# A graph layer with a gated update and a small expert layer: the weights' own product moved to the program's start, one gate's product moved at the first node tiles, and a new order for the last tile

## The chip, the cores and the metric

One Trainium2 chip, one of its cores. The metric is the time of one execution in microseconds (us); lower is better.

## What is computed

x has 10000 rows of 512; there are 2500 edges with 128 attributes each, sorted by destination. The reference, cut to what matters:

```python
hn = _layernorm(x)
m = relu(concatenate([hn[src], edge_attr], axis=1) @ W1.T + b1) @ W2.T + b2
agg = segment_sum(m, dst, num_segments=10000)
gi = agg @ W_ih.T + b_ih
gh = hn @ W_hh.T + b_hh
r = sigmoid(i_r + h_r); z = sigmoid(i_z + h_z); n = tanh(i_n + r * h_n)
h_new = (1.0 - z) * n + z * hn
x = x + hn + batchnorm(h_new)
h2 = _layernorm(x)
x = x + top2_of_8_experts(h2) + 0.5 * shared_expert(h2)
```

## The kernel before, in words

Every product keeps float32 accuracy with three matmuls: each operand is split into a high part (ScalarE, ACT, copies it to the fast format) and a low part (VectorE, DVE, subtracts), and TensorE (PE) multiplies high by high, high by low and low by high. One matmul of PE has 512 columns; a product over 512 inputs is 12 matmuls.

**Edges.** The 2560 padded edges are 20 tiles of 128, in 5 groups g of 4 tiles j. Per group: GpSimd (POOL) gathers the source rows (`gather_source`, L703), DVE takes their statistics (`stats`), POOL and ACT normalise them (`front`, `normalise`), PE turns them (`transposes`, L1271), ACT and DVE split them (`transposed_hi`, `transposed_lo`), PE makes the first layer (`layer1`, L1283, 60 matmuls per group), DVE adds b1 (`messages`), and PE sums edges of one destination with a 0/1 matrix (`sums`, L1334). W2 and W_ih are not applied one after the other: `fused_weights` (L1303) multiplies W2 by W_ih once, 3 thirds q of 4 tiles i by 12 matmuls, and b2 by W_ih, 3 times 12 matmuls. `product(g, j)` (L1352) multiplies the sums by the result and DVE adds what earlier tiles left (`take_gates`, L1031). `find` and `find_before` (L1035, L1039) search all destinations for each edge's own, `last_places` turns that into addresses. `keep_running` (L1371) issues turns of the identity, whose result nobody reads.

**Nodes.** 79 tiles t of 128 rows, a pipeline of periods (`periods`, L479): in period p, PE makes gates r, n and z of tile t, the expert layers of tiles t-1 (`f1`, 296 columns, 12 matmuls) and t-2 (7 matmuls of 512 columns). A chain runs from the z gate over DVE (five steps and the statistics, L1670 to L1680), POOL and ACT to the turn of tile t's rows by PE in the next period.

**What sets the order.** Each engine has its own instruction list, written out by hand, and runs it in order; semaphores (`wait_ge`) tie them. SP's list of DMA issues (L611 to L627) sets the order of the loads, POOL's list that of the gathers.

## Time and profile before

| | |
|---|---|
| three runs | 1315.44, 1317.50, 1317.52 us (median 1317.5) |
| profiled execution | 1315.33 us, its span 1313.5 us |
| PE busy | 1280.1 us (97%), 6360 matmuls |
| DVE, POOL, ACT busy | 997.5, 819.8, 732.8 us (76, 62, 56%) |
| mean DMA rate | 137 GB/s |

The busy time of PE is the time in which a matmul was under way; 97% leaves some 33 us of the span in which none was. In the page's 40 slices PE shows 6 tenths in the first, 5 in the last, and 8 or 9 in the others.

### The profile page before, as it was taken

What the parts mean: (1) busy time and instruction counts of PE and PEld (TensorE: products, weight loads), DVE (VectorE), ACT (ScalarE), POOL (GpSimd) and SP (SyncE); (2) the same over time, 40 slices, a digit from 0 to 9 for tenths busy, and PEclk for the clock granted to TensorE, in tenths of its full rate; (3) what the DMA queues carried; (4) which work ended last, traced back from release to release, by engine and by line L of the source; (5) the groups of instructions that cost most, each with busy time, mean ns of one, the idle gap of its engine ahead of it and who ended that gap; (6) DMA issues with size and microseconds to landing.
All of it is one profiled execution on the core that took longest, in us unless ns stands there. A gap on an engine that the chain in (4) does not pass through costs nothing. (4 is left out here: it accounts for less than half of the span.)

```text
span 1313.5 us, 22819 instructions
## 1 busy us (share of the span) xinstructions
PE 1280.1 (97%) x6360; PEld 1082.6 (82%) x6360; DVE 997.5 (76%) x2190; ACT 732.8 (56%) x1721; POOL 819.8 (62%) x1119
## 2 busy tenths in 40 slices
PE   6999999999899999999999999999999999999995
PEld 5788888888688888888888888888888888888884
DVE  6887666659687777778778778777777777877874
ACT  4420223124576666666666666666666666666652
POOL 4201152213787777777777777777778777777761
PEclk9999999999899999999999999999999999999998
DMA  8213554277434334334344343333333333433320
GB/s 328 59 33 113 177 211 172 112 276 241 144 122 132 132 126 134 123 128 136 120 131 133 122 138 123 129 135 126 132 125 128 136 120 130 134 121 136 126 97 33
DMA packets 62960, 179.58 MB, mean 137 GB/s; under 512 B 9360, under 2 KB 10000, under 8 KB 62800
## 3 DMA queue, kind: packets, MB, share of 16 engines
q1 hardware_dynamic: 46912, 99.20, 21.9%
q0 software_dynamic: 16016, 79.97, 18.0%
q8 instruction: 17, 0.28, 0.1%
q14 instruction: 15, 0.12, 0.0%
HBM read 141.86 MB, written 37.29 MB: 136 GB/s over the span
## 5 line engine op out<-in xcount | busy, mean ns | idle before, releaser
L1737 PE MATMUL bank<-whh_hi,x_hi 128*128 128x512 f32 x948 | 376.3, 397 | 0.4 <-DVE g_out L1029 0.4
L1737 PE MATMUL bank<-whh_hi,x_lo 128*128 128x512 f32 x948 | 369.9, 390 | 0.0
L1737 PE MATMUL bank<-whh_lo,x_hi 128*128 128x512 f32 x948 | 369.5, 390 | 0.0
L1737 PEld LDWEIGHTS bank<-whh_hi,x_lo 128*128 128x128 f32 x948 | 177.9, 188 | 37.9
L1737 PEld LDWEIGHTS bank<-whh_hi,x_hi 128*128 128x128 f32 x948 | 178.2, 188 | 35.8 <-issue 0.8
L1737 PEld LDWEIGHTS bank<-whh_lo,x_hi 128*128 128x128 f32 x948 | 178.3, 188 | 34.4
L1535 POOL TENSOR_TENSOR h_n<-h,n_gate 128x512 f32<-128x512 f32 x78 | 100.9, 1294 | 65.5 <-ACT n_gate L1586 65.5
L1467 POOL TENSOR_TENSOR rstd<-var_eps,minus_half 128x1 f32<-128x1 f32 x158 | 89.9, 569 | 66.9 <-DVE var_eps L499 66.9
L1634 DVE TENSOR_TENSOR h_lo<-bank,h_hi 128x512 fp32r<-128x512 f32 x79 | 54.6, 692 | 80.8 <-ACT h_hi L1577 80.8
L1452 POOL DMA_INDIRECT gates<-gates_in,slot_at x78 | 84.2, 1079 | 45.8 <-issue 45.8
L1529 POOL TENSOR_TENSOR n_pre<-r_hn,gates 128x512 f32<-128x512 f32 x78 | 100.5, 1288 | 13.2 <-POOL r_hn L1525 13.2
L1777 PE MATMUL bank<-f_hi,h_hi 128*128 128x296 f32 x316 | 102.1, 323 | 2.3 <-DVE h_lo L1634 2.3
L541 POOL TENSOR_TENSOR x_lo<-x_lo_raw,x_hi 128x512 fp32r<-128x512 f32 x77 | 100.7, 1308 | 2.9 <-ACT x_hi L535 0.4
L1517 POOL TENSOR_TENSOR x_h_b<-x_h,bn_shift 128x512 f32<-128x512 f32 x78 | 101.1, 1296 | 0.0
L1525 POOL TENSOR_TENSOR r_hn<-r_gate,hn 128x512 f32<-128x512 f32 x78 | 99.7, 1279 | 1.8 <-DVE hn L1610 1.3
L1777 PE MATMUL bank<-f_lo,h_hi 128*128 128x296 f32 x316 | 95.4, 302 | 0.0
...
L1777 PE MATMUL bank<-f_hi,h_lo 128*128 128x296 f32 x316 | 95.3, 301 | 0.0
L1366 PE MATMUL bank<-wih_hi,a_hi 128*128 128x512 f32 x240 | 93.9, 391 | 0.0
L1366 PE MATMUL bank<-wih_lo,a_hi 128*128 128x512 f32 x240 | 93.4, 389 | 0.0
L1366 PE MATMUL bank<-wih_hi,a_lo 128*128 128x512 f32 x240 | 93.4, 389 | 0.0
L1577 ACT ACTIVATE h_hi<-bank 128x512 fp32r<-128x512 f32 x79 | 47.4, 600 | 75.6 <-PE bank L546 75.5
...
## 6 DMA issues: line engine op xcount, KB each, us to landing
...
```

What stands on the lines that cost most here:

```text
L541: eng.tensor_tensor(x_lo[:, s, :], x_raw[:, s, :], x_hi[:, s, :].bitcast(F32), ALU.subtract)\
L1366: last = pe.matmul(to[0:R, :], a[:, k, j * R:(j + 1) * R], w[:, k, q * D:(q + 1) * D], start=n == 0, stop=n == 3 * DK - 1)
L1452: pool.indirect_dma_start(out=gates[:, s, :], out_offset=None, in_=gates_in, in_offset=bass.IndirectOffsetOnAxis(ap=slot_at[:, s:s + 1], a ...
L1467: pool.tensor_tensor(rstd[which][:, of:of + 1], var_eps[which][:, :], minus_half[0:R, 0:1], ALU.pow)\
L1517: pool.tensor_tensor(x_h_b[:, s, :], x_h[:, s, :], bn_shift[:, :], ALU.add).then_inc(x_h_b_done, 1)
L1525: pool.tensor_tensor(r_hn[:, :], r_gate[:, :], hn[:, s, :], ALU.mult).then_inc(r_hn_done, 1)
L1529: pool.tensor_tensor(n_pre[:, :], r_hn[:, :], gates[:, s, 2 * D:G3], ALU.add).then_inc(n_pre_done, 1)
L1535: pool.tensor_tensor(h_n[:, :], h[:, s, :], n_gate[:, s, :], ALU.subtract).then_inc(h_n_done, 1)
L1577: act.activation(h2_hi[:, :], b_th2[:, 0:DK * R], ACT.Copy).then_inc(h2_hi_done, 1)
L1634: dve.tensor_tensor(h2_lo[:, :], b_th2[:, 0:DK * R], h2_hi[:, :].bitcast(F32), ALU.subtract)\
L1737: last = pe.matmul(to[0:R, :], a[:, s, k * R:(k + 1) * R], w[:, k, q * D:(q + 1) * D], start=n == 0, stop=n == 3 * DK - 1)
L1777: last = pe.matmul(b_f1[0:R, 0:F1], a[:, k * R:(k + 1) * R], w[:, k, 0:F1], start=n == 0, stop=n == 3 * DK - 1)
```

## The change

Line numbers of the change are its own. It has three parts.

**Start.** PE's list begins with 12 turns of the identity and the product of the weights (its first third in quarters over k, each as its loads come), and the first edge rows are gathered, normalised and turned beside it; `fused_weights` is gone from its place behind `layer1(1)`. W2 and the first third of W_ih come in four quarters of 256 KB each, as SP's first loads; W1 comes last. POOL makes the identity first and gathers after the quarters have landed. PSUM banks are dealt out anew. ACT's and DVE's lists follow: the searches stand between other work, two of them ahead of the first rows' low parts. The waits on PE's list are new too.

**Third node tile.** Its 12 matmuls of gate r stand behind tile 1's gate z, ahead of the turning of tile 0's new rows, and no longer behind tile 0's first expert layer.

**Last tile.** DVE, not POOL, makes its r*hn and the sum before tanh; ACT makes its tanh ahead of two older steps; `best_two` and the choice of experts of tile 77 stand behind the last tile's chain, and the y of tile 76 one period later; PE turns the identity 25, 10 and 6 times between; the last 7 matmuls become 14 of 256 columns in two banks, and y is added and stored in halves.

DVE's list at the start, as it now stands:

```python
    for k in range(DK):
        quarters_lo(k)
    ...
    third_lo(1)
    for of in HALVES:
        stats(0, of)
    third_lo(2)
    fused_lo(0)
    dve.wait_ge(dst_in, 16)
    ...
    dve.wait_ge(all_dst_in, 16)
    ...
    dve.tensor_copy(all_dst[:, 0:E], all_dst_i[:, :]).then_inc(all_dst_done, 1)
    ...
    find(0)
    find(1)
    for j in range(SUP):
        transposed_lo(0, j)
    w1_lo_of(0, slice(0, 3))
    fused_lo(1)
    w1_lo_of(1, slice(3, K1))
    attributes_lo(0)
    stats(1)
    compare(0)
    fused_lo(2)
    messages(0, 0)
    ...
    find_before(0)
    messages(0, 1)
    messages_lo(0, 0)
    find_before(1)
    find_before(2)
    messages(0, 2)
    messages_lo(0, 1)
    messages(0, 3)
    messages_lo(0, 2)
    messages_lo(0, 3)
    attributes_lo(1)
    for j in range(SUP):
        transposed_lo(1, j)
    count(0)
    sums_lo(0)
    compare(1)
    messages(1, 0)
    find(2)
    messages(1, 1)
    messages_lo(1, 0)
    ...
```

ACT's list at the start up to the second group's messages, as it now stands:

```python
    for k in range(DK):
        act.wait_ge(fused_in[k], 32)
        hi_of(w2_hi[:, k, :], w2_raw[:, k, :]).then_inc(w_hi_done, 1)
        hi_of(wih_hi[:, k, 0:D], wih_raw[:, k, 0:D]).then_inc(wih_hi_done, 1)
    third_hi(1)
    act.wait_ge(b_in, 32)
    hi_of(b2_hi[:, :, :], b2_col[:, :].unsqueeze(2).broadcast_to((P, DK, P))).then_inc(w_hi_done, 1)
    third_hi(2)
    for of in HALVES:
        normalise(0, of)
    v_of(0)
    fused_hi(0)
    for n, at in enumerate((slice(0, 3), slice(3, K1))):
        act.wait_ge(w1_in[n], 16)
        hi_of(w1_hi[:, at, :], w1_raw[:, at, :]).then_inc(w_hi_done, 1)
    attributes_hi(0)
    for j in range(SUP - 1):
        transposed_hi(0, j)
    v_of(1)
    transposed_hi(0, SUP - 1)
    fused_hi(1)
    v_of(2)
    normalise(1)
    fused_hi(2)
    for j in range(SUP):
        messages_hi(0, j)
    attributes_hi(1)
    for j in range(SUP):
        transposed_hi(1, j)
    for f in range(DK):
        sums_hi(0, f)
    ...
```

The rest, cut to its core:

```diff
def bank_of_rows(g, j):
-        return bank[2 + (j if g < 2 else j % 2)]
+        return bank[((0, 1, 2, 0), (4, 5, 2, 3))[g][j] if g < 2 else 2 + j % 2]
+
+    def bank_of_units(g, j):
+        return bank[j % 2 + (6 if g == 0 else 0)]
...
@@ -609,22 +618,22 @@
     sp.dma_start(src_i[:, :], src).then_inc(src_in, 16)
+    for k in range(DK):
+        sp.dma_start(w2_raw[:, k, :], w2v[:, k, :]).then_inc(fused_in[k], 16)
+        sp.dma_start(wih_raw[:, k, 0:D], wihv[:, k, 0:D]).then_inc(fused_in[k], 16)
+    sp.dma_start(wih_raw[:, :, D:2 * D], wihv[:, :, D:2 * D]).then_inc(third_in[0], 16)
+    sp.dma_start(b2_col[:, :], b2).then_inc(b_in, 16)
+    sp.dma_start(b1_row[:, :], bcast(b1)).then_inc(b_in, 16)
+    sp.dma_start(wih_raw[:, :, 2 * D:G3], wihv[:, :, 2 * D:G3]).then_inc(third_in[1], 16)
+    sp.wait_ge(xs_in[SUP - 1], 16)
+    sp.dma_start(dst_i[:, :], dst).then_inc(dst_in, 16)
+    sp.dma_start(all_dst_i[:, :], dst_back.broadcast_to((R, E))).then_inc(all_dst_in, 16)
     sp.dma_start(w1_raw[:, 0:3, :], w1v[:, 0:3, :]).then_inc(w1_in[0], 16)
     sp.dma_start(m_raw[:, K1 - 1, :], attr_t[:, 0:SW]).then_inc(attr_in, 16)
     sp.dma_start(w1_raw[:, 3:K1, :], w1v[:, 3:K1, :]).then_inc(w1_in[1], 16)
-    sp.wait_ge(xs_in[SUP - 1], 16)
-    sp.dma_start(b1_row[:, :], bcast(b1)).then_inc(b1_in, 16)
-    sp.dma_start(dst_i[:, :], dst).then_inc(dst_in, 16)
-    sp.dma_start(w2_raw[:, :, :], w2v).then_inc(w2_in, 16)
     sp.dma_start(row_i[:, :], dst_rows[0:1, :].broadcast_to((R, SW))).then_inc(row_in, 16)
-    sp.dma_start(b2_col[:, :], b2).then_inc(b2_in, 16)
-    for k in range(2):
-        sp.dma_start(wih_raw[:, k, :], wihv[:, k, :]).then_inc(wih_in[k], 16)
     sp.dma_start(ig_bias[:, :], bcast(b_ih)).then_inc(bias_in, 16)
     sp.dma_start(ig_bhh[:, :], bcast(b_hh[0:2 * D])).then_inc(bias_in, 16)
-    for k in range(2, DK):
-        sp.dma_start(wih_raw[:, k, :], wihv[:, k, :]).then_inc(wih_in[k], 16)
-    sp.dma_start(all_dst_i[:, :], dst_back.broadcast_to((R, E))).then_inc(all_dst_in, 16)
...
-    pool.wait_ge(src_in, 16)
-    for j in range(SUP):
-        gather_source(0, j)
...
+    pool.wait_ge(src_in, 16)
+    pool.wait_ge(fused_in[DK - 1], 32)
+    for j in range(SUP):
+        gather_source(0, j)
...
+        if g == 0:
+            pe.wait_ge(fused_lo_done, DK)
+            if j == SUP - 1:
+                pe.wait_ge(t_lo, 1)
+        elif g == 1:
+            pe.wait_ge(fused_lo_done, 2 * DK if j < 2 else 3 * DK)
+        else:
...
+            if j < 2 and g == 0:
+                pe.wait_ge(fused_lo_done, 2 * DK)
+            elif j < 2:
+                pe.wait_ge(a_lo_done, DK * (g - 1) + j + 1)
+    def first_third():
+        for k in range(DK):
+            for n, (a, w) in enumerate(((w2_hi, wih_hi), (w2_hi, wih_lo), (w2_lo, wih_hi))):
+                if n == 0:
+                    pe.wait_ge(w_hi_done, k + 1)
+                    pe.wait_ge(wih_hi_done, k + 1)
+                if n == 1:
+                    pe.wait_ge(w_lo_done, k + 1)
+                    pe.wait_ge(wih_lo_done, k + 1)
+                for i in range(DK):
+                    last = pe.matmul(bank_of_fused(0, i)[:, :], a[:, k, i * P:(i + 1) * P], w[:, k, 0:D],
+                                     start=k == 0 and n == 0, stop=k == DK - 1 and n == 2)
+                    if k == DK - 1 and n == 2:
+                        last.then_inc(fused_prod, 1)
+    def third(q, tiles=range(DK)):
+        for i in tiles:
+            if i == 0:
+                pe.wait_ge(wih_lo_done, DK + q)
+            if q == 1 and i == DK - 1:
+                pe.wait_ge(fused_hi_done, 1)
+            if q == 2 and i == 0:
+                pe.wait_ge(t_lo, SUP)
+            if q == 2 and i == 2:
+                pe.wait_ge(fused_hi_done, 2 * DK + 3)
...
+    def bias_times_wih(q):
+        pe.wait_ge(w_lo_done, DK + 1)
+        if q > 0:
+            pe.wait_ge(wih_lo_done, DK + q)
+        if q == 1:
+            pe.wait_ge(fused_lo_done, DK)
+        if q == 2:
+            pe.wait_ge(t_lo, SUP - 1)
...
+        if g == 0:
+            pe.wait_ge(fused_lo_done, 3 * DK)
...
-    keep_running(14)
+    keep_running(12)
+    first_third()
+    bias_times_wih(0)
+    third(1)
+    for j in range(SUP - 1):
+        transposes(0, j)
+    bias_times_wih(1)
+    transposes(0, SUP - 1)
+    bias_times_wih(2)
+    third(2)
+    layer1(0)
     for j in range(SUP):
-        transposes(0, j)
-    keep_running(8)
-    layer1(0)
-    for j in range(2):
         transposes(1, j)
     sums(0)
-    for j in range(2, SUP):
-        transposes(1, j)
     layer1(1)
-    fused_weights()
     for j in range(SUP):
         product(0, j)
...
-    store(NT - 1, (NT - 1) % 2)
+    for n in range(2):
+        sp.wait_ge(y_done, NT + n)
+        sp.dma_start(out_tiles[:, NT - 1:NT, HALF[n]].rearrange("p o d -> p (o d)"),
+                     y[:, (NT - 1) % 2, HALF[n]]).then_inc(y_stored[(NT - 1) % 2], 16)
...
+    def last_new_gate(dve, p):
+        t, s = p.t, p.slot(1)
+        dve.wait_ge(r_done, t + 2)
+        dve.wait_ge(hn_done, t + 2)
+        dve.wait_ge(n_pre_done, t + 1)
+        dve.tensor_tensor(r_hn[:, :], r_gate[:, :], hn[:, s, :], ALU.mult).then_inc(r_hn_done, 1)
+        dve.wait_ge(n_done, t + 1)
+        dve.wait_ge(gates_loaded[s], 16 * (p.turn(1) + 1))
+        dve.wait_ge(r_hn_done, t + 2)
+        dve.tensor_tensor(n_pre[:, :], r_hn[:, :], gates[:, s, 2 * D:G3], ALU.add).then_inc(n_pre_done, 1)
...
+        if p.last(-1):
+            s = p.slot(-3)
+            dve.wait_ge(f2_prod, t - 2)
+            dve.wait_ge(y_stored[s], 16 * p.turn(-3))
+            dve.tensor_tensor(y[:, s, :], b_f2[0:R, :], x1[:, p.slot4(-3), :], ALU.add).then_inc(y_done, 1)
...
+        if p.last(0):
+            best_two(dve, p)
...
+            if p.last(1):
+                last_new_gate(dve, p)
+        if p.has(-2) and not p.last(0):
+            if p.last(-2):
+                for n, product in enumerate((b_f2, b_n)):
+                    dve.wait_ge(f2_prod, t - 1 + n)
+                    dve.tensor_tensor(y[:, s, HALF[n]], product[0:R, HALF[0]], x1[:, p.slot4(-2), HALF[n]],
+                                      ALU.add).then_inc(y_done, 1)
...
+    def second_layer(to, n, of):
+        for k in range(KF - 1):
+            for a, w in ((hid_hi, f2_hi), (hid_hi, f2_lo), (hid_lo, f2_hi)):
+                pe.matmul(to[0:R, 0:n], a[:, k * R:(k + 1) * R], w[:, k, of],
+                          start=k == 0 and a is hid_hi and w is f2_hi, stop=False)
+        last = pe.matmul(to[0:R, 0:n], hid_hi[:, (KF - 1) * R:KF * R], f2_hi[:, KF - 1, of],
+                         start=False, stop=True)
+        last.then_inc(f2_prod, 1)
+    def reset_gate(pe, p, k):
+        t, s = p.t + k, p.slot(k)
+        pe.wait_ge(x_lo_done, t + 1)
+        wait_from(pe, r_pre_done, t - 1)
+        gate(s, b_r[s], 0).then_inc(r_prod, 1)
+
     def body(p):
         t = p.t
         if p.has(0):
             s = p.slot(0)
-            pe.wait_ge(x_lo_done, t + 1)
-            wait_from(pe, r_pre_done, t - 1)
-            gate(s, b_r[s], 0).then_inc(r_prod, 1)
+            if not p.first(-2):
+                reset_gate(pe, p, 0)
             wait_from(pe, hn_done, t)
             gate(s, b_n, 2).then_inc(n_prod, 1)
         if p.has(0):
             if p.first(-1):
                 gate(p.slot(0), z_bank(p), 1).then_inc(z_prod, 1)
+
+                reset_gate(pe, p, 1)
...
+        if p.last(-1):
+            keep_running(10)
...
+            if p.last(-2):
+                second_layer(b_f2, D // 2, HALF[0])
+                second_layer(b_n, D // 2, HALF[1])
+            else:
+                second_layer(b_f2, D, slice(0, D))
+        if p.last(0):
+            pe.wait_ge(hn_done, NT)
+            pe.wait_ge(h_new_done, NT)
+            keep_running(8)
+            pe.wait_ge(x1_done, NT)
+            keep_running(6)
+            pe.wait_ge(var_done[2], NT)
+            keep_running(11)
+        if p.last(-1):
+            keep_running(6)
```

PE's list at the program's start. Before (ident is the identity, xs the gathered rows, w and m the first layer's operands):

```order
L1374 MATMUL bank<-ident 128x128 x14
L1279 MATMUL bank<-ident,xs 128x128 x16
L1374 MATMUL bank<-ident 128x128 x8
L1298 MATMUL bank<-w_hi,m_hi 128x512
L1298 MATMUL bank<-w_lo,m_hi 128x512
```

Now (wih and w are W_ih and W2):

```order
L1425 MATMUL bank<-ident 128x128 x12
L1344 MATMUL bank<-wih_hi,w_hi 128x512 x4
L1344 MATMUL bank<-wih_lo,w_hi 128x512 x4
L1344 MATMUL bank<-wih_hi,w_lo 128x512 x4
L1344 MATMUL bank<-wih_hi,w_hi 128x512 x4
```

The first layer and the turning of rows gave their place to 48 matmuls on weights alone, in four quarters of three such groups.

DVE's list around the first rows' low parts (m_lo). Before:

```order
L937 TENSOR_TENSOR w_lo<-w_lo_raw,w_hi 128x1024
L937 TENSOR_TENSOR m_lo<-m_lo_raw,m_hi 128x512
L962 TENSOR_TENSOR m_lo<-bank,m_hi 128x4x128 x4
L937 TENSOR_TENSOR w_lo<-w_lo_raw,w_hi 128x2048
L1116 CAST dst_f<-dst_i 128x20
L1117 CAST gval<-dst_i 128x8x2
L988 TENSOR_TENSOR msg_lo_raw<-bank,b_row 128x512
```

Now (wih_lo<-bank is the low part of the weights' product, found a search's result):

```order
L954 TENSOR_TENSOR wih_lo<-wih_lo_raw,wih_hi 128x4x512
L1024 TENSOR_TENSOR wih_lo<-bank,wih_hi 128x512 x4
L1143 CAST dst_f<-dst_i 128x20
L1144 CAST gval<-dst_i 128x8x2
L1148 CAST all_dst<-all_dst_i 128x2560
L1149 COPY all_dst<-dst_f 128x20
L1060 MAX_INDEX found<-dst_f,all_dst 128x8 x2
L986 TENSOR_TENSOR m_lo<-bank,m_hi 128x4x128 x4
L954 TENSOR_TENSOR w_lo<-w_lo_raw,w_hi 128x1536
```

The destinations' cast over 2560 columns and two searches stand ahead of the first m_lo now; the messages are far behind.

PE's list at its end, from the last whole period's second layer. Before:

```order
L1787 MATMUL bank<-f_hi,hid_lo 128x512
L1789 MATMUL bank<-f_hi,hid_hi 128x512
L546 MATMUL bank<-ident,h_169 128x128 x4
L546 MATMUL bank<-ident,hid 128x128 x3
L1777 MATMUL bank<-f_hi,h_hi 128x296
L1777 MATMUL bank<-f_lo,h_hi 128x296
```

Now (b_n takes the turns of the identity):

```order
L1857 MATMUL bank<-f_hi,hid_lo 128x512
L1859 MATMUL bank<-f_hi,hid_hi 128x512
L1852 MATMUL bank<-ident 128x128 x25
L552 MATMUL bank<-ident,h_169 128x128 x4
L1852 MATMUL bank<-ident 128x128 x10
L552 MATMUL bank<-ident,hid 128x128 x3
L1907 MATMUL bank<-f_hi,h_hi 128x296
L1907 MATMUL bank<-f_lo,h_hi 128x296
```

Twenty-five turns of the identity stand where the list had none, and ten more stand between the last tile's turn and that of hid.

## Rows read from the trace of the kernel before

**Rows 1.** Waits of PE over the whole span: total us, times, longest
```profile
PE bank L546 <- ACT h L1568: 10.3, 3, 5.5
PE bank L1374 <- POOL minus_half L746: 9.3, 1, 9.3
PE bank L1346 <- DVE msg_lo L993: 1.3, 1, 1.3
```

**Rows 2.** Windows: length, busy us (x) of PE, PEld, DVE, ACT, POOL, clock, DMA, GB/s
```profile
0.00:17.60 17.60, 6.93 (x38) 6.06 (x39) 7.80 (x19) 8.70 (x11) 10.96 (x27) 1.00 0.71 244
34.20:322.00 287.80, 287.60 (x1356) 240.97 (x1356) 205.78 (x317) 74.00 (x128) 57.53 (x65) 1.00 0.43 151
338.80:348.90 10.10, 4.22 (x17) 3.84 (x17) 5.04 (x10) 5.25 (x12) 7.30 (x9) 0.66 0.37 130
348.90:1289.30 940.40, 940.05 (x4775) 798.79 (x4774) 742.31 (x1776) 622.12 (x1528) 725.65 (x993) 1.00 0.38 126
1289.30:1302.50 13.20, 6.89 (x27) 5.85 (x26) 7.13 (x20) 2.82 (x11) 1.01 (x3) 0.74 0.05 20
```

**Rows 3.** Timeline of the first weight load, one window's rate, a DMA issue to landing
```profile
1.18 0.42 SPq L612 DMA_DIRECT2D w_lo_raw<-in_w1t  x1
...
5.78 1.48 ACT L809 ACTIVATE w_hi<-w_lo_raw 128x1536 fp32r<-128x1536 f32 x1 [3.76 <-DMA w_lo_raw<-in_w1t]
...
6.00:8.00 2.00, 0.00 (x0) 0.00 (x0) 0.71 (x1) 1.39 (x2) 1.58 (x3) 1.00 1.06 421
...
all_dst_i<-in_dst_back SPq DMA_DIRECT2D x1, 1280.0 KB, 18.9
```

**Rows 4.** Timeline of PE at the start: start us, us, instruction [idle before]
```profile
9.26 3.25 PE L1374 MATMUL bank<-ident 128*128 128x128 f32 x14 [9.26 <-POOL minus_half L746]
...
30.88 0.39 PE L1298 MATMUL bank<-w_lo,m_hi 128*128 128x512 f32 x1
31.11 0.39 PE L1298 MATMUL bank<-w_hi,m_lo 128*128 128x512 f32 x1
```

**Rows 5.** Timeline of DVE: rows' low parts, the destinations' cast and one search
```profile
16.79 2.48 DVE L962 TENSOR_TENSOR m_lo<-bank,m_hi 128x512 fp32r<-128x512 f32 x4 [2.30 <-ACT m_hi L825]
...
71.33 1.49 DVE L1164 CAST all_dst<-all_dst_i 128x2560 f32<-128x2560 int32 x1
...
73.13 2.82 DVE L1036 FIND_INDEX8 found<-dst_f,all_dst 128x8 uint32<-128x2560 f32 x1
```

**Rows 6.** Timeline of PE, POOL and DVE at the first node tiles
```profile
338.45 1.29 POOL L541 TENSOR_TENSOR x_lo<-x_lo_raw,x_hi 128x512 fp32r<-128x512 f32 x1
...
343.19 1.11 PE L546 MATMUL bank<-ident,h 128*128 128x128 f32 x4 [4.37 <-ACT h L1568]
...
347.18 1.29 POOL L1535 TENSOR_TENSOR h_n<-h,n_gate 128x512 f32<-128x512 f32 x1 [0.74 <-ACT n_gate L1586]
...
350.23 0.68 DVE L1670 TENSOR_TENSOR bank<-bank,h_n 128x512 f32<-128x512 f32 x1
```

**Rows 7.** Timeline of PE, ACT and DVE over the last tiles
```profile
1285.91 0.38 PE L1777 MATMUL bank<-f_hi,h_hi 128*128 128x296 f32 x1
...
1294.94 1.12 PE L546 MATMUL bank<-ident,h 128*128 128x128 f32 x4 [5.53 <-ACT h L1568]
...
1297.47 0.61 PE L1777 MATMUL bank<-f_hi,h_hi 128*128 128x296 f32 x1 [0.77 <-DVE h_lo L1634]
...
1286.58 0.62 ACT L1586 ACTIVATE n_gate<-n_pre 128x512 f32<-128x512 f32 x1
...
1287.83 0.47 DVE L1653 TENSOR_TENSOR bank<-bank,f_bias 128x296 f32<-128x296 f32 x1 [0.68 <-PE bank L1777]
...
1288.95 0.68 DVE L1670 TENSOR_TENSOR bank<-bank,h_n 128x512 f32<-128x512 f32 x1
...
1300.84 0.47 DVE L1653 TENSOR_TENSOR bank<-bank,f_bias 128x296 f32<-128x296 f32 x1 [3.09 <-PE bank L1777]
...
1307.77 0.69 DVE L1725 TENSOR_TENSOR y<-bank,x 128x512 f32<-128x512 f32 x1 [2.00 <-PE bank L1789]
```

318 lines of the change are left out of this document (147 added, 171 removed).

## The prediction

> **What bounds the kernel now.** I read the waits of TensorE (PE) first, then busy time by stretch, then timelines of the three places that the change touches. From 34.2 to 322 us PE had 287.6 of 287.8 us busy, and from 348.9 to 1289.3 us 940.05 of 940.4 [rows 2]: there the time is PE's own work, which the change keeps. What it can give back are the places where PE has nothing to do. There are three [rows 1, 2]: the start (idle to 9.26 us, then dummy turns and short waits), the first node tiles (338.8 to 348.9 us: 4.2 of 10.1 us busy, mean clock 0.66), and the last tile (from 1289.3 us: 6.9 of 13.2 busy, clock 0.74). The sum is made against the profiled execution, 1315.33 us; 0.2%, about what a measurement of this kernel can tell from no change, is 2.6 us.
>
> **The start, before.** The first first-layer matmul starts at 17.6 us. Ahead of it PE did one useful thing, 16 turns of 128 columns. Fourteen dummies took 3.25 us, 0.23 each [rows 4]; the second of the two levels, 2.4 GHz against 1.2, is twice as fast, so the 16 are worth about 1.6 us. Lost: 17.6 - 1.6 = 16.0 us. A later wait for msg_lo, between the rows' turning and the sums, adds 1.3 [rows 1].
>
> **The start, after.** PE's real work begins once a quarter of W2 and of W_ih is there and split. The first load of before, 768 KB, was issued at 1.18 us and its reader began at 5.78; the rate was then 421 GB/s [rows 3]. A quarter pair is 512 KB in two issues, 256 KB less: 0.6 us earlier, 5.1 us. ACT then makes two high parts of 512 columns at 0.6 each (n_gate, the same shape, took 0.62 [rows 7]): PE starts at 6.3 us. The further pairs come every 512 KB / 421 GB/s = 1.25 us, ACT needs 1.2 for one, DVE as much (four m_lo of 512 columns took 2.48, 0.62 each [rows 5]), PE 12 x 0.227 = 2.7 us (matmuls of 512 columns start 0.23 apart [rows 4]): PE is the slowest, so after its first quarter it should not wait. PE started at 9.26 on the lower level before; now the dummies start at about 2 us, since POOL makes the identity before the gathers. After the pause at 343 us the lower level lasted until the next stretch, some 6 us [rows 2, 6]; so I take it until 8 us: half of 8 - 6.3, 0.9 us, is lost. Lost at the start: 7.2 us in place of 16.0, a gain of 8.8.
>
> Eight loads now stand where one stood. The Trainium skill ("DMA: Bandwidth & Descriptors", section "Anatomy of one DMA — SWDGE (gpsimd) path") gives each DMA about 2.0 us fixed plus its bytes at 436 GB/s. The trace speaks against paying the fixed part one after the other: three loads of 1.5 MB issued within 1.4 us kept 421 GB/s between 6 and 8 us [rows 3]. By that page's figures, paid serially, the fourth pair would land at about 22 us; the same mechanism, priced from rows, is rival B.
>
> **New waits of the start.** PE has 48 + 12 + 48 matmuls (24.5 us) ahead of its first row turns: it comes to them at 6.3 + 0.9 + 24.5 = 31.7 us. Gathers, statistics and normalisation of the first rows were done before 17.6 us; starting 6 us later, they end by about 24, hidden. The gathers' DMAs pass behind 2 MB of quarters and beside 2 MB of thirds: at 421 GB/s all of it is in by about 17 us. SP waits for the last gather, then issues the destinations' table (1280 KB, 3.1 us at that rate), in by about 22; W1 follows by 27 and is needed from 37. DVE has about 27 us of work and waits until the product's first low parts are made (after ACT's copies, which stand behind the rows' normalisation); then the cast, 1.5, and two searches, 2.8 each [rows 5], to 34.3, then the rows' low parts, 0.6 each: the third at 36.2. PE has made three tiles' turns, b2's second product (2.7) and the fourth tile's turn by 35.9 and waits for that third part with b2's third product: 0.3 to 0.9, I take 0.5. The sums of the first group wait for the last message's low part as before, with 16 turns ahead of them and not 8: 0.8 in place of the 1.3. The next first layer follows the sums at once; its bank waits for DVE's a_lo, behind four m_lo, a count and the attributes, whose load can only be issued when the first layer is done: 0.4. No wait in the products: DVE's rest there (12 double additions, 4 searches, 4 m_lo, `last_places`) is some 32 us beside 33 us of PE, and four banks let PE lead by 10 us. Start in all: 8.8 + 1.3 - 1.7 = **8.4 us**. Bounds: 10 with no new wait and the quarters 0.6 sooner; 4 with the quarters 3 us later and double waits.
>
> **The third node tile.** PE waited 4.37 us for tile 0's new rows, until 343.19. The third tile's x_lo ends at 339.74 [rows 6], so its 12 matmuls (2.7 us) fit in from 339.8 to 342.6. What they free behind the first expert layer is PE's time, though, and the next bound is the chain: POOL's h_n of tile 1 starts at 347.18 for 1.29 us, whatever PE does, and DVE's step on it, at 350.23 before, can start at 348.5 [rows 6]. PE then waits for tile 1's chain twice. So of 2.7 us and of what the higher clock gives (the first expert layer at half the time), 350.23 - 348.5 = **1.7 us** comes through. Bounds: -0.5, if the clock falls in the new pauses, and 2.7.
>
> **The last tile.** DVE needs 0.7 for each of the two steps that POOL took 1.29 for (h_n shows POOL's rate [rows 6]); it can begin when ACT has r. Two such steps are 1.2 us shorter, and ACT's tanh, at 1286.58 before, can be at 1285.1, behind h_hi; but DVE's z_pre slips behind y and h_lo (0.7 each, three in a row from 1285.0), so the sigmoid on it ends at about 1287.7 and the chain starts at 1287.75 in place of 1288.95 [rows 7]: 1.2. PE's turn of the new rows comes at 1293.7, not 1294.94. From there to the first expert matmul were 2.53 us, at the lower clock (four turns 1.12); kept awake by dummies, with DVE's hid of tile 77 now ahead of h_lo, about 2.35: 1296.05 in place of 1297.47. Twelve matmuls and the hand-over to DVE took 3.37 us at the lower clock and 1.92 in the period before [rows 7]: DVE's bias starts at 1297.97 in place of 1300.84, 2.87 us sooner. From there to y the work is the same. Halving the 7 matmuls changes no columns; the last addition has 256 columns, about half of 0.69 [rows 7], so 0.3 less, and the last store half the bytes, 0.1: **3.3 us**. The dummies cost nothing while they fit into the pauses: 25 x 0.1 us between 1289.7 and 1293.7, 10 behind the turn beside 1.9 us of ACT and DVE; at 0.23 each the ten would delay the product by 0.3 to 0.8. Bounds: 0.5 and 4.5.
>
> **Sum.** 8.4 + 1.7 + 3.3 = 13.4: 1315.33 - 13.4 = 1301.9 us for an execution like the profiled one. The median of the runs lies 2.2 above it, two of three at 1317.5; between the two I put the new median at 1302.5.
>
> **Rivals.**
> - A, dummies that do not keep the clock. They fill about half of the pause, and nothing in the trace shows dummies holding it; before, the turns at 1294.94, after 5.5 us of nothing, were slow (1.12 for four) [rows 7]. If it falls, the product is at half speed as before and ten cold dummies stand ahead of it: the last tile gives 1.2 - 0.5 + 0.4 = 1.1: 1304.7. The Trainium skill ("TensorE: Matmul & The Clock Gate", section "What's actually happening") says that the gate follows how busy PE has been lately, which would favour the dummies.
> - B, quarters paid one after another, each pair 5.1 - 1.2 = 3.9 us: the fourth lands at 16.8 us, PE ends the first third at 20.7 in place of 18.1, and the second third, 4.6 us for its load and 4.4 for its parts, keeps PE waiting for 2.4 more: 5 us, 1307.5. Against it stands the rate [rows 3].
> - C, slower: the table of destinations lands late. DVE's list holds the cast ahead of everything that PE needs from the rows. The place is the third part for which b2's third product waits. From about 27 us on, each us of delay is one of the whole. Before, this load took 18.9 us to land, with some 6 MB queued ahead [rows 3]; issued at 18 it would be in at 37, which costs 10: 1312.5. Past 43 us the change is slower than before, at 45 it gives 1320. Against it: 17 us is when the queue ahead is empty.
> - D, more than forecast: no new wait, quarters early, whole r product saved: 10 + 2.7 + 4.5 = 17.2, 1298.7.
>
> **Chances.** Forecast with its bounds 0.72, A 0.10, B 0.05, C 0.08 (0.04 of it slower than before), D 0.05. Faster by over 0.2%: 0.93; within 0.2%: 0.03; slower: 0.04. The range reaches from just under D past B, to a table that lands 7 us late (C): 1298 to 1309.5.
>
> **What would show it.** Right: PE's first product matmul at 6 to 7 us and no idle over 1 us in it; L1374's wait of 9.3 us gone, waits of under 1 us for m_lo, msg_lo and a_lo; no r product behind the first expert layer, h_n of tile 1 followed by DVE at once, and PE waits of 1 to 2 us in the third tile; clock 1.00 from the last turn to the end. Wrong: a wait of PE for m_lo over 2 us (C), the second quarter's matmuls waiting for ACT (B), clock 0.5 in the last expert layer (A), or PE's stretch of products no longer full.

## The result, and the profile after

| | kernel before | changed kernel |
|---|---|---|
| median of runs | 1317.16 us (5 runs, 1315.44 to 1317.52) | 1305.45 us (5 runs, 1303.76 to 1308.08) |
| ratio after / before | | 0.9916, 95% interval 0.9898 to 0.9933 |
| profiled execution, and its span | 1315.33, 1313.5 us | 1303.76, 1301.9 us |

The change is 11.7 us faster by the medians and 11.6 by the profiled executions, where 15.0 (from the three runs' median of 1317.5 to 1302.5) and 13.4 were forecast. The new runs lie 4.3 us apart, and the profiled one is the fastest of them.

Waits of TensorE (PE) in the changed kernel (us in total, times, longest), which answer to [rows 1]:

```profile
PE bank L552 <- ACT h L1648: 2.1, 3, 1.4
PE bank L1344 <- ACT wih_hi L820: 2.1, 1, 2.1
PE bank L1907 <- DVE h_lo L1733: 2.0, 2, 1.5
PE bank L1844 <- DVE x L1774: 1.6, 1, 1.6
PE bank L552 <- POOL hid L1569: 1.5, 2, 1.2
PE bank L1378 <- DVE m_lo L986: 0.6, 1, 0.6
PE bank L1306 <- DVE m_lo L986: 0.3, 1, 0.3
```

The wait of 10.3 us for h is 2.1, the one of 9.3 us for the identity has gone, and two small waits for m_lo are new. The windows of the changed kernel (length, PE busy, clock, DMA share, GB/s) answer to [rows 2]:

```profile
0.00:17.60 17.60, 13.98 (x53) 1.00 0.90 307
34.00:60.00 26.00, 25.09 (x114) 1.00 0.15 43
330.00:350.00 20.00, 14.68 (x72) 1.00 0.33 109
1280.00:1297.00 17.00, 12.83 (x90) 1.00 0.09 36
```

The clock column tells nothing of the time before the first rise; from there it holds 1.00 to the last product, through the places where it was 0.66 and 0.74 [rows 2]. The timeline of PE (start, us, instruction, idle before it) shows the start; its first rows answer to [rows 4]:

```profile
1.54 2.82 PE L1425 MATMUL bank<-ident 128*128 128x128 f32 x12 [1.54 <-POOL minus_half L752]
6.45 2.04 PE L1344 MATMUL bank<-wih_hi,w_hi 128*128 128x512 f32 x4 [2.09 <-ACT wih_hi L820]
8.29 1.91 PE L1344 MATMUL bank<-wih_lo,w_hi 128*128 128x512 f32 x4
10.00 1.18 PE L1344 MATMUL bank<-wih_hi,w_lo 128*128 128x512 f32 x4
...
37.39 0.63 PE L1306 MATMUL bank<-ident,xs 128*128 128x128 f32 x4 [0.34 <-DVE m_lo L986]
38.59 0.47 PE L1378 MATMUL bank<-wih_hi,b_hi 128*128 128x512 f32 x1 [0.57 <-DVE m_lo L986]
```

The eight first products take 1.84 and 1.71 us per four, as on the lower level; from 10.0 on four start within 1.0, then 0.91. From the node stage and the tail, rows that answer to [rows 6, 7], first DVE's (VectorE's) steps on the first tiles and on tile 77 in the kernel before, then the changed kernel's:

```profile
327.98 0.75 DVE L1610 SCALAR_TENSOR_TENSOR hn<-bank,rstd,hn_bias 128x512 f32<-128x512 f32 x1 [0.48 <-PE bank L1737]
...
337.17 0.70 DVE L1670 TENSOR_TENSOR bank<-bank,h_n 128x512 f32<-128x512 f32 x1
...
1276.74 0.68 DVE L1670 TENSOR_TENSOR bank<-bank,h_n 128x512 f32<-128x512 f32 x1
```
```profile
321.16 0.75 DVE L1685 SCALAR_TENSOR_TENSOR hn<-bank,rstd,hn_bias 128x512 f32<-128x512 f32 x1 [1.16 <-PE bank L1844]
...
329.82 0.70 DVE L1766 TENSOR_TENSOR bank<-bank,h_n 128x512 f32<-128x512 f32 x1
...
341.25 0.70 DVE L1766 TENSOR_TENSOR bank<-bank,h_n 128x512 f32<-128x512 f32 x1
...
1267.78 0.68 DVE L1766 TENSOR_TENSOR bank<-bank,h_n 128x512 f32<-128x512 f32 x1
...
1285.00 0.65 PE L552 MATMUL bank<-ident,h 128*128 128x128 f32 x4 [0.33 <-ACT h L1648]
1285.49 1.25 PE L1852 MATMUL bank<-ident 128*128 128x128 f32 x10
1287.05 0.52 PE L552 MATMUL bank<-ident,hid 128*128 128x128 f32 x3 [0.31 <-POOL hid L1569]
...
1289.24 0.47 DVE L1710 TENSOR_TENSOR bank<-bank,f_bias 128x296 f32<-128x296 f32 x1 [0.68 <-PE bank L1907]
...
1294.23 0.39 PE L1857 MATMUL bank<-f_hi,hid_hi 128*128 128x256 f32 x1 [1.04 <-DVE hid_lo L1752]
```

Where the 11.6 us came from, by the same instructions in both profiles: the node stage's first step on DVE (line 1685) starts at 321.16 instead of 327.98, so the start gave 6.8. DVE's step on tile 0's h_n is at 329.82 instead of 337.17, 7.35 sooner. That further 0.5 is no part of the change at the third tile: DVE waited 1.72 us for the gates of its first tile to land, and 2.49 before. The step on tile 1's h_n, 350.23 [rows 6], is at 341.25, 8.98 sooner: the third tile gave 1.6. Tile 77's step is 8.96 sooner, so the tiles between gave nothing. The last bias addition went from 1300.84 [rows 7] to 1289.24, 11.6 sooner: the last tile gave 2.6, and nothing behind it gave anything.

### The profile page after: what moved, and what is told of

Same layout as the page of the kernel before. It is cut to its first block and busy times, and to the rows that moved or that the text cites. A ratio compares the mean times of both kernels' runs of the same rounds, so it can differ in the third digit from the quotient of the medians.

```text
span 1301.9 us, 22928 instructions
## 1 busy us (share of the span) xinstructions
PE 1281.2 (98%) x6398; PEld 1083.2 (83%) x6398; DVE 997.7 (77%) x2198; ACT 734.0 (56%) x1726; POOL 816.4 (63%) x1117
## 5 line engine op out<-in xcount | busy, mean ns | idle before, releaser
L1844 PEld LDWEIGHTS bank<-whh_lo,x_hi 128*128 128x128 f32 x948 | 178.3, 188 | 34.3
L1575 POOL TENSOR_TENSOR x_h_b<-x_h,bn_shift 128x512 f32<-128x512 f32 x78 | 101.2, 1297 | 0.0
## 6 DMA issues: line engine op xcount, KB each, us to landing
whh_lo_raw<-in_whh_t SPq DMA_DIRECT2D x4, 768.0 KB, 10.3
```

The costliest lines, as they stand in the source:

```text
L1575: pool.tensor_tensor(x_h_b[:, s, :], x_h[:, s, :], bn_shift[:, :], ALU.add).then_inc(x_h_b_done, 1)
L1844: last = pe.matmul(to[0:R, :], a[:, s, k * R:(k + 1) * R], w[:, k, q * D:(q + 1) * D], start=n == 0, stop=n == 3 * DK - 1)
```

## The experiments

Medians of 4 to 6 runs of each, beside runs of before on the same chip (three groups of four; the kernel before had 1317.15, 1316.59 and 1316.64 in them):

| run | median (lowest to highest) | ratio to before, 95% | clock down near 40 us / in the third tile's stretch, in its profile |
|---|---|---|---|
| e1 start undone | 1311.66 (1310.59 to 1313.20) | 0.9958 (0.9945 to 0.9972) | no / yes |
| e2 tail undone | 1308.46 (1306.65 to 1310.02) | 0.9932 (0.9919 to 0.9946) | yes / yes |
| e3 third r back | 1307.13 (1305.34 to 1308.76) | 0.9923 (0.9910 to 0.9937) | yes / yes |
| e4 transposes in the middle | 1306.53 (1304.94 to 1308.56) | 0.9920 (0.9906 to 0.9933) | yes / no |
| e5 changed kernel again | 1305.98 (1304.83 to 1307.41) | 0.9920 (0.9907 to 0.9932) | no / no |
| e6 searches behind | 1305.05 (1302.86 to 1306.16) | 0.9906 (0.9892 to 0.9921) | no / yes |
| e7 e4 and e6 together | 1302.89 (1301.56 to 1305.34) | 0.9899 (0.9884 to 0.9915) | no / no |
| e8 no transposes in the tail | 1307.82 (1306.05 to 1310.66) | 0.9932 (0.9920 to 0.9945) | yes / yes |
| e9 e7 and more at the start | 1302.51 (1301.19 to 1304.87) | 0.9895 (0.9877 to 0.9912) | no / no |
| e10 whole loads | 1307.57 (1307.22 to 1309.42) | 0.9935 (0.9921 to 0.9949) | no / no |
| e11 third's low part later | 1309.31 (1308.21 to 1310.51) | 0.9947 (0.9933 to 0.9960) | yes / yes |
| e12 last layer whole | 1304.66 (1304.33 to 1308.27) | 0.9914 (0.9898 to 0.9930) | yes / no |

The medians alone do not tell two of these versions apart when they are less than about 2 us apart: the interval of each ratio is 1.6 to 2.3 us to either side, and e1 to e4, e5 to e8 and e9 to e12 ran on three different chips. The profiles can say more, since the same stretch can be measured in each of them. The columns, in us: DVE's first step of the node stage (when it starts), from there to its step on tile 0's h_n, from tile 0's to tile 1's, from tile 1's to tile 77's, and from tile 77's to PE's first product of the last layer.

| profile | start | to tile 0 | third tile | tiles 1 to 77 | last tile |
|---|---|---|---|---|---|
| before | 327.98 | 9.19 | 13.06 | 926.5 | 29.09 |
| changed kernel | 321.16 | 8.66 | 11.43 | 926.5 | 26.45 |
| e1 | 328.10 | 9.31 | 12.54 | 927.7 | 26.04 |
| e2 | 323.27 | 9.01 | 12.64 | 926.5 | 29.07 |
| e3 | 323.58 | 8.47 | 13.10 | 927.7 | 26.41 |
| e4 | 323.55 | 9.45 | 11.46 | 927.7 | 26.41 |
| e5 | 321.63 | 9.26 | 11.45 | 927.7 | 26.45 |
| e6 | 320.29 | 9.76 | 12.51 | 927.7 | 26.41 |
| e7 | 318.31 | 9.09 | 11.47 | 927.7 | 26.42 |
| e8 | 323.46 | 8.62 | 12.64 | 927.7 | 28.75 |
| e9 | 318.50 | 8.98 | 11.44 | 927.7 | 26.42 |
| e10 | 324.51 | 9.13 | 11.44 | 926.5 | 26.41 |
| e11 | 325.36 | 8.21 | 12.17 | 926.5 | 26.41 |
| e12 | 322.82 | 9.10 | 11.45 | 927.7 | 26.42 |

The fifth column is a surprise: the 76 tiles in which PE is always busy take 926.5 us in five profiles and 927.7 in nine, at a clock of 1.00 in both, and the changed kernel has been seen with either. No experiment touched that, and its cause is open.

**e1: the start of before, with the other two parts.** The file before, with the node stage of after and its two helpers (`HALF`, `last`).

> The kernel before with the new third node tile and the new last tile, and with its own start. The two profiles give the three parts of the gain as 6.8 us (start), 2.15 us (third node tile) and 2.6 us (last tile). Theory 1, the parts stand by themselves: 4.7 us below the kernel before, about 1312.4 us, and the turn of the second tile's h at about 354 us instead of 356.2. Theory 2, the part of the start is worth the 8.4 us of the prediction and the other two are smaller than the profiles say (3.2 us together): about 1314 us. Theory 3, the later parts only pay with the new start, because the clock falls somewhere else: above 1315 us.

It ran in 1311.66 us: the other two parts are worth 5.5 us beside their own runs of before, the start 5.7 to 6.2 (to 1305.98 and 1305.45). The median is nearest to theory 1 (1312.4), so the two parts stand without the start. Its sign did not come, though: the turn of the second tile's h is at 355.96 and not at 354. In this profile the clock fell in the third tile's stretch, and that part gave 0.5 (12.54 against 13.06) and not 1.6. What the medians miss of the forecast lies mostly in the start: its 8.4 are some 6.

**e2: the old tail.**
```diff
         def last(self, k):
-            return isinstance(self.i, int) and self.t + k == NT - 1
+            return False
```
and the store of before.

> The changed kernel with the old order of the last tiles: no early choice on ScalarE, the last new gate's products on GpSimd, no transposes to keep TensorE running, the last layer and the store in one piece. Theory 1, the last tile is worth the 2.6 us that the profiles show: 1308.0 us. Theory 2, it is worth the predicted 3.3 us: 1308.8 us. Theory 3, most of it was the clock, which falls in the old tail's pause of 5.5 us and not in the new one: then the granted clock here drops before the last turns, and the last expert matmul starts 1.4 us or more after the last turn instead of the 1.2 to 2.3 us of a full clock with its dummies.

1308.46 us, 2.5 above e5 by the medians and 1.6 by the ratios, which leaves theories 1 and 2 open. The profile decides for theory 1: its last tile takes 29.07 us, as before (29.09), against 26.45. The clock also did what theory 3 says, with PE's wait of 5.53 us for h back and the four turns at 1.11:

```profile
1289.62 1.11 PE L552 MATMUL bank<-ident,h 128*128 128x128 f32 x4 [5.53 <-ACT h L1645]
```

**e3: the third tile's r at its old place.**
```diff
-                    if not p.first(-2):
-                        reset_gate(pe, p, 0)
+                    reset_gate(pe, p, 0)
...
-                        reset_gate(pe, p, 1)
```

> The changed kernel with the r product of the third node tile back behind the first tile's expert layer. Theory 1, the worth of moving it is the 2.15 us that the profiles show (predicted 1.7 us): 1307.6 us, and TensorE waits some 4 us for the first h. Theory 2, the chain of the second tile bounded the stretch in any case: within 0.5 us of the changed kernel, 1305.5 us. The clock should fall again in the longer pause, in nearly every run, which would make the runs of this kernel agree more closely than the changed kernel's five, which lie 4.3 us apart.

1307.13 us: 1.2 above e5 and 1.7 above the changed kernel's first median, 0.4 and 0.9 by the ratios. That decides between the theories as little as the intervals do. The profile does: with r at its old place, DVE's steps on tile 0's and tile 1's h_n are 13.10 us apart, as before (13.06), against 11.43 with r moved.

```profile
332.05 0.70 DVE L1766 TENSOR_TENSOR bank<-bank,h_n 128x512 f32<-128x512 f32 x1
...
345.15 0.68 DVE L1766 TENSOR_TENSOR bank<-bank,h_n 128x512 f32<-128x512 f32 x1
```

So the move is worth 1.6 to 1.7 us where the clock holds, and both theories were off. Where it falls in spite of the move (e1, e2, e6, e8, e11), the distance is 12.17 to 12.64, and the move is worth 0.4 to 0.9. PE waits 3.66 us for the first h, the window from 330 to 350 us has a clock of 0.83, and the second wait has shrunk to 0.25. The runs do not agree more closely (3.4 us apart), so the spread is not made there alone. The profile shows another place, which e2's and e4's show too: near 40 us, behind a wait for m_lo.

**e4: transposes in the middle.**
```diff
+            def fill_pause(n):
+                for _ in range(n):
+                    pe.transpose(b_thid[:, 0:P], ident[:, :], ident[:, :])
...
+                if p.first(-1):
+                    fill_pause(13)
...
+                        if p.first(-2):
+                            fill_pause(14)
                         wait_from(pe, x1_done, t)
                         gate(p.slot(0), b_z, 1, 0, 2)
+                        if p.first(-2):
+                            fill_pause(13)
```

> The changed kernel with 13, 14 and 13 transposes of the identity in three of the four pauses that TensorE still has in the third node tile's stretch (1.5, 1.6 and 1.4 us long), into the bank of the hidden units, which is free there. The changed kernel's five runs lie between 1303.8 and 1308.1 us, with mean granted clocks from 0.999 to 0.995. Theory 1, the slower ones are those in which the clock fell in these pauses: all runs here at 1303.5 to 1304.5 us. Theory 2, it falls at the start or in the tail: the same spread as before, median about 1305.4 us. Theory 3, the transposes delay the products behind them: all runs up by 0.3 to 1 us.

Theory 1 is refuted as the whole cause: the clock held in the middle, and the time did not move (0.9920, as e5). The profiled run, 1308.06 us, was over 4 slower than the changed kernel's, with no pause of PE left in the middle but 1.14 and 0.47 us. It had lost 2.4 us at the start, 0.8 until tile 0's step and 1.1 in tiles 1 to 77; the third tile took 11.46, so the transposes cost nothing there. The start's part shows in the windows of PE from 34 to 60 us, of e4 and, below it, of e3:

```profile
34.00:60.00 26.00, 23.75 (x99) 0.93 0.15 43
```
```profile
34.00:60.00 26.00, 23.74 (x99) 0.93 0.15 44
38.34 0.63 PE L1306 MATMUL bank<-ident,xs 128*128 128x128 f32 x4 [1.70 <-DVE m_lo L986]
```

0.07 of 26 us is 1.8 us, beside the 25.09 us busy at clock 1.00 in the changed kernel's profile.

**e5: the changed kernel once more.**

> The changed kernel itself, for its runs beside the others of this group on one chip. Its first five runs lay between 1303.8 and 1308.1 us. The three profiles of its variants show two places where a run can lose: TensorE's wait for the first m_lo (0.34 us in the changed kernel's profile, 1.22, 1.70 and 1.69 us in those of the variants) with a fall of the clock near 41 us behind it in those three and not in the changed kernel's own, and a fall near 342 us. Theory: the middle run has one of the two, so a median of 1305 to 1307 us again, a lowest near 1303.8, and where this profile has a wait of over 1 us for m_lo it also has the fall.

As expected in the median; its profile had the wait of over 1 us (1.17) without the fall. So the two are not one thing. Ordered by that first wait for m_lo: 0.34 and 1.17 us (the changed kernel, e5) without a fall, 1.22, 1.69, 1.70, 1.96 and 2.24 us (e2, e4, e3, e8, e12) with one.

The two profiles of this one kernel are 2.3 us apart: 0.5 at the start, 0.6 until tile 0's step and 1.1 in tiles 1 to 77, none of it a fall of the clock. The rows of tiles 1 and 77 in e5:

```profile
342.34 0.70 DVE L1766 TENSOR_TENSOR bank<-bank,h_n 128x512 f32<-128x512 f32 x1
...
1270.00 0.68 DVE L1766 TENSOR_TENSOR bank<-bank,h_n 128x512 f32<-128x512 f32 x1
```

Why m_lo is late is in DVE's timeline of e5 (and, with the same order, in all of them): from 27.10 us on it never waits until the searches are done.

```profile
27.10 2.48 DVE L1024 TENSOR_TENSOR wih_lo<-bank,wih_hi 128x512 fp32r<-128x512 f32 x4 [3.39 <-ACT wih_hi L862]
...
31.65 2.82 DVE L1060 FIND_INDEX8 found<-dst_f,all_dst 128x8 uint32<-128x2560 f32 x1
...
34.44 2.82 DVE L1060 FIND_INDEX8 found<-dst_f,all_dst 128x8 uint32<-128x2560 f32 x1
...
39.29 0.69 DVE L986 TENSOR_TENSOR m_lo<-bank,m_hi 128x512 fp32r<-128x512 f32 x1 [0.24 <-ACT m_hi L836]
```

**e6: the two searches behind.**
```diff
-            find(0)
-            find(1)
             for j in range(SUP):
                 transposed_lo(0, j)
...
             compare(0)
+            find(0)
+            find(1)
             fused_lo(2)
```

> The changed kernel with VectorE's two searches of 2.8 us each moved from before the four m_lo to behind the comparison of the first four tiles, where VectorE idles 3.8 us for ScalarE. Theory 1, VectorE's list ahead of m_lo bounds TensorE in every run (0.9 us of waits in the changed kernel's profile, 2.3 us in the profiles of two variants) and the fall of the clock near 41 us (1.7 us) comes from that wait: both go, the median falls by 1 to 3 us to 1302.5 to 1304.5 us and lies under the changed kernel's. Theory 2, the waits come from the rows (ScalarE's m_hi) and not from the searches: no change. Theory 3, the searches now push the third third's low parts (54.1 us in the changed kernel's profile) back by more than VectorE's idle time in front of them: TensorE waits before the first sums instead, and nothing is won.

Both waits for m_lo are gone; from its first product to 70 us PE waits once for another engine, 0.38 us for a message. So the searches were what m_lo waited for; theory 2 is out. The node stage starts at 320.29, 0.9 and 1.3 us sooner than in the changed kernel's two profiles. The median fell by 0.9, its ratio to before by 0.0014 (1.8 us); the intervals overlap, so a gain in the whole time is not shown by this run alone. Not all of it arrives: the node stage's third tile now waits longer for GpSimd's (POOL's) x_lo, 1.54 instead of 0.95 us in e5, and the clock fell in the middle of this profile (0.91 from 330 to 350 us).

**e7: e4 and e6 together.**

> The searches behind, and the transposes in the three pauses of the third node tile's stretch. If the two falls of the clock are all that spreads the runs, these five agree within 1.5 us and their median is the lowest of all, 1302 to 1303.5 us. If the transposes themselves cost time, this is slower than the kernel with the searches behind alone by what they cost; the profile of the variant with the transposes alone had 0.47 us of waits left in the stretch, so less than 0.7 us.

1302.89 us, the lowest median so far, but the spread is still 3.8 and not under 1.5: the two falls of the clock are not all that spreads the runs. Its profile holds the clock from the first product to the last, also over the first eight:

```profile
6.14 1.17 PE L1344 MATMUL bank<-wih_hi,w_hi 128*128 128x512 f32 x4 [1.78 <-ACT wih_hi L820]
7.14 1.09 PE L1344 MATMUL bank<-wih_lo,w_hi 128*128 128x512 f32 x4
...
329.93 0.50 PE L1844 MATMUL bank<-whh_hi,x_hi 128*128 128x512 f32 x1 [0.78 <-POOL x_lo L547]
333.43 0.66 PE L552 MATMUL bank<-ident,h 128*128 128x128 f32 x4 [0.48 <-ACT h L1648]
```

With the same twelve transposes the first eight products took 3.55 us in the changed kernel's profile (6.45 to 10.00) and 1.93 here (6.14 to 8.07): 1.6 us. So when the clock first rises differs from run to run, and e4's profiled run had lost near 40 us more than it kept later; whether that is why e4's median did not fall, no profile of its other four runs tells.

**e8: no transposes in the tail.**
```diff
-                    keep_running(10)
+                    keep_running(0)
```
and the same for 8, 6, 11 and 6.

> The changed kernel without any of its 41 transposes of the identity in the last tile (10, 8, 6, 11, 6 become 0). Theory of the prediction: they only hold the clock; without them the pause of some 5 us before the last turns takes the clock to its lower level, and rows at either level (turns of the last h 1.11 against 0.66 us, six products of the z gate and twelve of the expert layer at half speed) make it 1.5 to 2.5 us slower. Rival: the transposes stand in the way of real work (the turn of the hidden units stands behind ten of them, 0.3 us) and the clock would hold without them: 0.3 us faster.

1307.82 us, 1.8 above e5 (1.6 by the ratios), as the prediction's reading has it. The four turns behind the 3.97 us of waiting take 1.09, and the clock over 1280 to 1297 us is 0.80:

```profile
1280.00:1297.00 17.00, 11.13 (x53) 0.80 0.08 31
1289.81 1.09 PE L552 MATMUL bank<-ident,h 128*128 128x128 f32 x4 [3.97 <-ACT h L1648]
```

By the profiles the transposes carry 2.3 of the tail's 2.6 us (28.75 against 26.45, and 29.09 before), which leaves 0.3 for the gate on DVE and the new order.

**e9: e7, and 18 transposes ahead of the first product.**
```diff
-            keep_running(12)
+            keep_running(18)
```

> The kernel with the searches behind and the transposes in the middle, and 18 instead of 12 transposes of the identity ahead of the first product, so that TensorE idles about 0.4 us there and not 1.8. In one profile of that kernel the clock was at its upper level from the first product (four products in 1.17 us), in all others it rose only near 10 us (four products in 2.05, the next four 1.75 to 1.91), which costs 1.1 us (18.29 against 17.14 for the end of the first third). Theory 1, the pause between the transposes and the first product decides it: the profile has the upper level from the first product, the runs agree more closely, median 1302 to 1302.5 us. Theory 2, when the clock rises is a matter of the phase at which the run starts: the spread stays, median 1302.9 us as without, and this profile may show either.

1302.51 us. (The expectation's price was read off wrongly: the first third of the changed kernel's profile ends where b2's product starts, at 19.20 and not 18.29, against 17.14.) The profile has the upper level from the first product, as e7's has with 12; the spread did not shrink (3.7 us). Inconclusive: e11 and e12, with 12, had the upper level there too, e10 at its late start not. Which of the theories holds stays open. Six of the eight runs of e7 and e9 are below the fastest of the changed kernel's ten (1303.76), and e9 is the fastest version here.

**e10: whole loads.**
```diff
-            for k in range(DK):
-                sp.dma_start(w2_raw[:, k, :], w2v[:, k, :]).then_inc(fused_in[k], 16)
-                sp.dma_start(wih_raw[:, k, 0:D], wihv[:, k, 0:D]).then_inc(fused_in[k], 16)
+            sp.dma_start(w2_raw[:, :, :], w2v[:, :, :]).then_inc(fused_in[0], 16)
+            sp.dma_start(wih_raw[:, :, 0:D], wihv[:, :, 0:D]).then_inc(fused_in[0], 16)
```

> The changed kernel with W2 and the first third of W_ih loaded by one DMA each instead of four, with the same splitting into high and low parts behind them. Theory 1, the quarters' overlap is what puts the first product at 6.4 us: all 2 MB land at about 9.2 us (when the fourth quarter does now), the first product starts at 10.3 to 10.5 us, and since TensorE has no other work, the kernel loses most of the 4 us, less what the later waits for m_lo (0.9 to 2.5 us) give back: 1307.5 to 1309.5 us. Theory 2, each DMA has a cost that adds to the queue, so two large ones land clearly sooner than 9.2 us, and the loss is under 1.5 us.

```profile
9.19 0.63 ACT L819 ACTIVATE w_hi<-w_lo_raw 128x512 fp32r<-128x512 f32 x1 [7.17 <-DMA wih_lo_raw<-in_wih_t]
...
10.48 2.05 PE L1343 MATMUL bank<-wih_hi,w_hi 128*128 128x512 f32 x4 [6.12 <-ACT wih_hi L819]
```

The 2 MB are in at 9.19 us. In the changed kernel ACT took up the four pairs of quarters at 5.15, 6.51, 7.77 and 9.15: six DMAs more cost nothing. PE starts 4.0 us later, and the kernel loses 1.6 by the medians (to e5), at the lower end of theory 1. PE waits nowhere between 10.48 and 70 us. How much of the 4 us arrives depends on what the run beside it lost: the node stage starts 3.4 and 2.9 us later than in the two profiles of the changed kernel (waits for m_lo of 0.91 and 1.74 us, no fall), but only 0.9 to 1.7 later than in e2, e3, e4, e8 and e12, where the clock fell behind that wait.

**e11: the third third's low part behind the four m_lo.**
```diff
-            third_lo(2)
             fused_lo(0)
...
             for j in range(SUP):
                 transposed_lo(0, j)
+            third_lo(2)
             w1_lo_of(0, slice(0, 3))
```

> The changed kernel with one step of VectorE moved: the low part of the third third of W_ih (2.28 us) behind the four m_lo instead of ahead of the first third's low parts. GpSimd's power for the second half of the first rows took 2.67 us beside it, 0.74 us without. Theory 1, the two engines hinder each other and this power is a link of the chain to the first m_lo: it takes 0.7 to 0.8 us here, the first third's low parts and the first m_lo come about 1.9 us sooner, TensorE's wait for m_lo goes, median 1304 to 1305 us. Theory 2, the long power is GpSimd's own: it stays at 2.67 us, and nothing moves.

The power behind the second half's statistics, of the changed kernel and of e11:

```profile
21.00 2.67 POOL L739 TENSOR_TENSOR rs_e<-ve_e,minus_half 128x2 f32<-128x2 f32 x1 [0.77 <-DVE ve_e L967]
```
```profile
22.03 0.70 POOL L739 TENSOR_TENSOR rs_e<-ve_e,minus_half 128x2 f32<-128x2 f32 x1 [0.76 <-DVE ve_e L967]
...
36.45 0.63 PE L1306 MATMUL bank<-ident,xs 128*128 128x128 f32 x4 [1.56 <-DVE m_lo L986]
40.73 0.77 PE L1378 MATMUL bank<-wih_hi,b_hi 128*128 128x512 f32 x1 [3.66 <-DVE wih_lo L954]
```

Theory 1 holds for the power, which takes long beside that step of DVE and is a link of the chain to m_lo: DVE's low parts of the weights' product start at 25.56 (26.50 in the changed kernel), and the m_lo come 0.95 us sooner, half of the 1.9 expected. The first wait for m_lo did not go: PE, whose first product was at 5.90 and on the upper level, came to it sooner. The kernel got slower by 3.3: I had not counted that b2's third product needs the part that I moved, and PE waits 3.66 us for it, with a clock of 0.87 from 34 to 60 us.

**e12: the last layer, its addition and its store whole.**
```diff
-                    if p.last(-2):
-                        second_layer(b_f2, D // 2, HALF[0])
-                        second_layer(b_n, D // 2, HALF[1])
-                    else:
-                        second_layer(b_f2, D, slice(0, D))
+                    second_layer(b_f2, D, slice(0, D))
```

> The changed kernel with the last tile's last layer, its addition and its store in one piece again. The prediction gave the halves 0.4 us (0.3 the addition, 0.1 the store); the profile of the changed kernel has the last addition end 0.24 us sooner behind the same last matmul and the stores take 0.24 us longer. Theory 1, they are worth nothing: within 0.3 us of the changed kernel, 1305.5 to 1306 us, with about 5.0 us from the last addition to the end. Theory 2, the predicted 0.4 us is there: 1306.2 us, with the end of the store as with the halves, 5.3 us.

1304.66 us; by ratio (0.9914 against 0.9920) the same. The rows of the first product of the last layer and of DVE's last addition, in the changed kernel (span 1301.9), e5 (1304.2) and e12 (1305.2):

```profile
1294.23 0.39 PE L1857 MATMUL bank<-f_hi,hid_hi 128*128 128x256 f32 x1 [1.04 <-DVE hid_lo L1752]
1296.20 0.42 DVE L1828 TENSOR_TENSOR y<-bank,x 128x256 f32<-128x256 f32 x1 [0.31 <-PE bank L1859]
```
```profile
1296.45 0.50 PE L1857 MATMUL bank<-f_hi,hid_hi 128*128 128x256 f32 x1 [1.04 <-DVE hid_lo L1752]
1299.76 0.42 DVE L1828 TENSOR_TENSOR y<-bank,x 128x256 f32<-128x256 f32 x1 [0.97 <-PE bank L1859]
```
```profile
1297.45 0.50 PE L1848 MATMUL bank<-f_hi,hid_hi 128*128 128x512 f32 x1 [1.04 <-DVE hid_lo L1749]
1300.16 0.69 DVE L1822 TENSOR_TENSOR y<-bank,x 128x512 f32<-128x512 f32 x1 [2.77 <-PE bank L1850]
```

In e5 and e12 the clock fell during this layer (0.63 and 0.66 from 1297 to 1301 us), so the last addition ends 3.7 and 3.4 us behind the layer's first product, against 2.4 in the changed kernel. Yet from that first product to the end of the span are 7.67, 7.75 and 7.75 us. It is 7.66 to 7.79 in all fourteen profiles, that of before included (7.67). Whatever ends the span there, it is not the last products, the addition or the store, if they are up to 1.3 us late. What it is, no run settled.

## Why the prediction was right and where it was off

Faster by over 0.2% was the forecast (0.93), and the time, 1305.45, is in the range; the forecast itself, 1302.5, was 3 us too low. All three places gave by the mechanism foreseen; two of the three sizes were too large. That the profiled run is within 1.9 us of its forecast is in part luck: it was one of the better runs. By its own steps, first for the profiled execution (1301.9 forecast, 1303.76 measured):

- **Start, 8.4, measured 6.8.** PE's first product was put at 6.3 and came at 6.45; the stretch of products has no wait (24.55 us busy from 6.45 to 31.00), as forecast; the serial payment of rival B did not occur (e10; the figures of 2.0 us and 436 GB/s that the prediction quotes on this are given for DMAs that GpSimd issues, and these are SP's). Off were two steps. "So I take it until 8 us": the lower level lasted to 10.0, so b2's first product, forecast for 18.1, came at 19.20. And "two searches ... to 34.3 ...: the third at 36.2": the searches ended at 36.58 and the third part at 38.44. I had listed DVE's own work and not the chain beside it: the second third's landing, its parts, the statistics, POOL's power (2.67 us where the one before it took 0.74), ScalarE's normalisation and its copies of the first product. The wait of 0.5 for m_lo was 0.34 + 0.57 here and 1.74 in e5. Where the clock fell behind it, the start gave 4.4 to 5.2 (e2, e3, e4, e8, e12).
- **Third node tile, 1.7, measured 1.6** in the profiles; e3's median cannot tell. The mechanism held: the next bound was tile 1's chain, with PE waiting 1.56 and 1.43 us. POOL's h_n of tile 1 started at 347.18 "whatever PE does", and so it is: 10.01 us behind DVE's step on tile 0's h_n before, 10.04 now (339.86). Another 0.5 us came ahead of it, from gates that landed sooner; it was in no term. The bounds had the clock in mind: where it fell, 0.4 to 0.9 was left.
- **Last tile, 3.3, measured 2.6** (and 2.6 in e2's profile). The chain started 1.0 sooner instead of 1.2, the first expert matmul 1.2 instead of 1.4, the bias 2.6 instead of 2.9. The last 0.4, "0.3 less, and ... 0.1" for the halves, is nothing (e12). Rival A's price for a clock that does not hold, 2.2, is 2.3 in e8's profile and 1.8 by its median. The Trainium skill ("TensorE: Matmul & The Clock Gate", section "What's actually happening") spoke for the transposes, and the trace agrees: clock 1.00 with them, 0.80 without.
- **From the profiled execution to the median, 0.6, measured 1.7.** "Between the two I put the new median": this step failed too. I took the small spread of the runs of before for that of the new kernel, and did not ask what would differ between runs of the new kernel. Three things do: the wait for m_lo moved between 0.34 and 2.24 us; behind it, in the third tile's stretch and at the start the clock was down or up from profile to profile; and tiles 1 to 77 took 926.5 or 927.7 us. The profiled run of the changed kernel had the short wait, no fall after the first rise, and the 926.5.
- Rival C named the right place (DVE's list ahead of m_lo, each microsecond one of the whole) and the wrong cause: the table landed in time, the list itself was long. Its sign, a wait for m_lo of over 2 us, came once, in e12 (2.24), without its cause. e6, which takes the searches out of the list, has no wait for m_lo at all.
